# Splitting four state steps of a scan into three fp32r passes, and moving three pieces of work between engines

## The reference, cut to what matters

```
x[t] = A^T x[t-1] + B^T u[t]          u = layernorm(h), t = 0..511 in each sequence
c[t] = max |x[t]| over a head's 64 states
y[t] = (x[t] * e^2 / c[t]) C + u[t] D
```

## Time and profile before

| | us |
|---|---|
| median of 3 executions (lowest, highest) | 171.67 (171.63, 171.71) |
| the profiled execution's own time | 171.82 |
| its span | 170.1 |
| PE busy in the span | 161.4 |
| DVE, ACT, POOL busy | 127.9, 102.1, 101.8 |

### The profile page before, as it was taken

The page is one execution under the profiler, slowest core; times in us unless marked ns, Lnnn a source line. Parts: engine busy times, 40 slices in busy tenths (PEclk is TensorE's granted clock), DMA queues, the critical chain, the costliest instruction groups (busy, mean ns, idle before and its releaser), DMA issues.

```text
span 170.1 us, 3494 instructions
## 1 busy us (share of the span) xinstructions
PE 161.4 (95%) x1165; PEld 138.8 (82%) x1165; DVE 127.9 (75%) x403; ACT 102.1 (60%) x238; POOL 101.8 (60%) x168
## 2 busy tenths in 40 slices
PE   5988989999999999999999989999999999989992
PEld 1676875887766799987679889999999999979991
DVE  3969959833338384897994997989979898649883
ACT  3048999462134532423435857959779597788991
POOL 5337687669997035361313694996979969785000
PEclk9999999999999999999999999999999999999999
DMA  4996000000000000000000000010010100110022
GB/s 144 354 428 287 4 0 2 0 6 0 0 0 0 4 0 0 0 6 0 0 0 0 4 0 0 0 67 0 0 67 0 64 4 0 62 62 6 0 105 82
DMA packets 2182, 7.47 MB, mean 44 GB/s; under 512 B 238, under 2 KB 748, under 8 KB 1908
## 3 DMA queue, kind: packets, MB, share of 16 engines
q1 hardware_dynamic: 2146, 7.23, 11.2%
q10 hardware_dynamic: 18, 0.02, 0.1%
HBM read 5.15 MB, written 2.10 MB: 43 GB/s over the span
## 4 chain that ended last, share of the span: by engine, by line
PE 83%; ACT 5%; POOL 4%; DVE 3%; issue 3%; DMA 1%; POOLq 0%; ACTq 0%; DVEq 0%
PE bank L1347 12%; PE bank L1327 12%; PE bank L1276 8%; PE bank L1191 6%; PE bank L1185 5%; PE bank L1273 4%; PE bank L1056 4%; PE bank L1106 4%; PE bank L1081 4%; PE bank L1296 4%; PE bank L1112 3%; PE bank L1303 2%; POOL rstd L521 2%; PE bank L1029 2%; POOL hid_p L538 2%
## 5 line engine op out<-in xcount | busy, mean ns | idle before, releaser
L538 POOL TENSOR_TENSOR hid_p<-hid_f,hid_p 128x256 fp32r<-128x256 f32 x48 | 34.2, 736 | 13.6 <-ACT hid_p L696 13.6
L694 ACT ACTIVATE hid_f<-bank,pa 128x256 f32<-128x256 f32 x64 | 30.8, 492 | 16.0 <-PE bank L1327 14.1
L1327 PE MATMUL bank<-xaT_p,fc_p 128*128 128x256 f32 x192 | 35.1, 294 | 0.2 <-issue 0.2
L1347 PE MATMUL bank<-hid_p,out_hi 128*128 128x256 f32 x128 | 32.5, 290 | 1.0 <-POOL hid_p L538 1.0
L1327 PEld LDWEIGHTS bank<-xaT_p,fc_p 128*128 128x128 f32 x192 | 26.7, 190 | 0.4 <-issue 0.4
L1347 PEld LDWEIGHTS bank<-hid_p,out_hi 128*128 128x128 f32 x128 | 23.4, 188 | 2.0 <-POOL hid_p L538 1.4
L696 ACT ACTIVATE hid_p<-bank,pa 128x256 fp32r<-128x256 f32 x48 | 23.4, 488 | 0.0
L1276 PE MATMUL bank<-pb,xh 128*128 128x128 f32 x128 | 19.5, 275 | 0.0
L521 POOL TENSOR_TENSOR rstd<-spread,neg_half 128x8 f32<-128x8 f32 x8 | 13.6, 1697 | 9.5 <-DVE spread L966 9.5
L1347 PE MATMUL bank<-hid_p,out_lo 128*128 128x256 f32 x64 | 17.9, 279 | 0.0
L1276 PEld LDWEIGHTS bank<-pb,xh 128*128 128x128 f32 x128 | 16.9, 192 | 0.0
(11 more groups left out here) (161 smaller groups left out, 375.7 us busy)
## 6 DMA issues: line engine op xcount, KB each, us to landing
fc_w<-in_fc SPq DMA_DIRECT2D x2, 2048.0 KB, 11.4
out<-res SPq DMA_DIRECT2D x7, 256.0 KB, 2.0
pa<-in_pack_a SPq DMA_DIRECT2D x1, 407.0 KB, 3.2
pb<-in_pack_b SPq DMA_DIRECT2D x1, 384.0 KB, 4.5
out<-res SPq DMA_DIRECT2D x2, 128.0 KB, 1.7
pw<-in_pack_a SPq DMA_DIRECT2D x1, 64.0 KB, 3.1
emb_w<-in_emb SPq DMA_DIRECT2D x1, 62.5 KB
conv_w<-in_conv ACTq DMA_DIRECT2D x1, 1.0 KB
```

What stands on the lines that cost most here:

```text
L538: nc.gpsimd.tensor_tensor(hid_p[1][:, half, c, :], hid_f[:, m % HID_SLOTS, :], hid_p[0][:, half, c, :].bitcast(F32), ALU.subtract).then_in ...
L694: full = nc.scalar.activation(hid_f[:, m % HID_SLOTS, :], src, ACT.Gelu, bias=bias)
L1327: last = mm(fc1_bank(8 * b + n)[:, 0:HALF], fc1_p[w][:, e * HID + c * P:e * HID + (c + 1) * P], xaT_p[m][:, b % 2, half, :], start=(k == 0 ...
L1347: last = mm(out_bank(b, half)[:, half * HALF:(half + 1) * HALF], out_p[w][:, e, c * CH:(c + 1) * CH], hid_p[m][:, half, c, :], start=(c == ...
```

## The change

It does five things. (1) Group 0's state steps with q >= 1 (n = 2 to 5) become three fp32r passes; their low-part pass alone waits for the low part of the state. (2) For this ACT copies the bank of states 0 to 3 twice, first to a high part, then to X; DVE subtracts the low part from X; A is split once (ACT high, DVE low). The parts lie in slots of `out_hi` and `out_lo` that fused weights fill later. (3) u's four high parts of group 1 go from POOL to ACT, ahead of `next_starts`. (4) DVE's four `split_low` of group 1 are interleaved with the four `state_low`. (5) `fuse(3)` goes from behind group 0's state steps to between the second and the third of them; its copies on ACT go behind the second state copy.

```
-            -3: (("fuse",), ("run", "run"), ("run", "run"), ("fuse",), ...
+            -3: ((), ("run", "run"), ("run", "run"), ("fuse",), ...
# POOL
-                pool.wait_ge(fc1_split, NE)
-                pool.wait_ge(uT_ready, NB)
-                for b in range(GB):
-                    nc.gpsimd.tensor_copy(u_split(1, 0)[:, b], uT[:, GB + b]).then_inc(u_hi[1], 1)
# ACT
                 def copy_state(g, n):
                     q, a = divmod(n, NP)
                     act.wait_ge(state_done[g], n + 1)
+                    if g == 0 and q < RUN - 2:
+                        nc.scalar.activation(state_split(a, 0), scan_bank(a), ACT.Copy).then_inc(s_hi, 1)
                     nc.scalar.activation(every_run(g, a, q + 1), ..., ACT.Copy).then_inc(x_ready[g], 1)
...
+                split_a()
                 copy_out_prep(N_PREP - 1)
                 copy_runs(1, 0)
                 for e in range(2, FUSED_FRONT):
                     copy_fused(e)
+                act.wait_ge(fc1_split, NE // 2)
+                for b in range(GB):
+                    nc.scalar.activation(u_split(1, 0)[:, b], uT[:, GB + b], ACT.Copy).then_inc(u_hi[1], 1)
                 next_starts(0)
                 for n in range(NP * (RUN - 1)):
                     copy_state(0, n)
+                    if n == NP - 1:
+                        copy_fused(FUSED_FRONT)
# DVE
                 def split_low(g, b):
                     dve.wait_ge(u_hi[g], b + 1)
+                    if g == 1:
+                        dve.wait_ge(fc1_split, NE)
...
-                for n in range(GB):
-                    split_low(1, n)
+                def state_low(n):
+                    q, a = divmod(n, NP)
+                    dve.wait_ge(s_hi, n + 1)
+                    dve.wait_ge(x_ready[0], n + 1)
+                    nc.vector.tensor_tensor(state_split(a, 1)..., every_run(0, a, q + 1),
+                                            state_split(a, 0)..., ALU.subtract).then_inc(s_lo, 1)
+                dve.wait_ge(a_hi, 1)
+                nc.vector.tensor_tensor(a_split(1), a1, a_split(0).bitcast(F32), ALU.subtract).then_inc(a_lo, 1)
+                state_low(0)
+                state_low(1)
+                split_low(1, 0)
+                state_low(2)
+                split_low(1, 1)
+                state_low(3)
+                split_low(1, 2)
+                split_low(1, 3)
# PE
-                    mm(scan_bank(a), a1, every_run(g, a, q), start=False, stop=True).then_inc(state_done[g], 1)
+                    if g == 0 and q >= 1:
+                        pe.wait_ge(a_lo, 1)
+                        pe.wait_ge(s_hi, n - 1)
+                        for k, (w, m) in enumerate(PARTS):
+                            if m == 1:
+                                pe.wait_ge(s_lo, n - 1)
+                            last = mm(scan_bank(a), a_split(w), state_split(a, m), start=False, stop=(k == len(PARTS) - 1))
+                    else:
+                        last = mm(scan_bank(a), a1, every_run(g, a, q), start=False, stop=True)
+                    last.then_inc(state_done[g], 1)
...
                 state_step(0, 1)
+                fuse(FUSED_FRONT)
                 for n in range(NP, NP * (RUN - 1)):
                     state_input(0, n)
                     state_step(0, n)
```

More of the change, by code:

```diff
@@ L227, in build @@
         next_ready = [sem(f"next_ready{g}") for g in range(NG)]
+        a_hi, a_lo, s_hi, s_lo = sem("a_hi"), sem("a_lo"), sem("s_hi"), sem("s_lo")
         full_ready = sem("full_ready")
@@ L312, in u_runs_split, with state_split, a_split @@
             return u_split(g, part)[:, :, q:q + T - RUN + 1:RUN, :]
+        def state_split(a, part):
+            return out_p[1][:, NE - 2 * NP + 2 * a + part, :]
+        def a_split(part):
+            return out_p[0][:, NE - 1, part * P:(part + 1) * P]
         def b_split(part, a, n):
@@ L338, in build @@
         PLAN = {
-            -3: (("fuse",), ("run", "run"), ("run", "run"), ("fuse",), ("carry",), ("fuse",), (), (), ()),
+            -3: ((), ("run", "run"), ("run", "run"), ("fuse",), ("carry",), ("fuse",), (), (), ()),
             -2: (("carry",), ("carry",), ("carry", "fuse"), ("carry",), ("input", "carry"), (), ("carry", "input"),
@@ L357, in numbered @@
         def numbered(plan):
-            done, out = dict(fuse=FUSED_FRONT, run=RUN, carry=0, input=0, step=0), {}
+            done, out = dict(fuse=FUSED_FRONT + 1, run=RUN, carry=0, input=0, step=0), {}
             for j, places in plan.items():
@@ L606, in split_high, with split_a @@
                         nc.scalar.activation(u_split(0, 0)[:, b], uT[:, b], ACT.Copy).then_inc(u_hi[0], 1)
+                def split_a():
+                    nc.scalar.activation(a_split(0), a1, ACT.Copy).then_inc(a_hi, 1)
                 act.wait_ge(ld_pa, 32)
@@ L865, in _ @@
                         fused_lo((3, 4, 8).index(n))
-                for n in range(GB):
-                    split_low(1, n)
+                def state_low(n):
+                    q, a = divmod(n, NP)
+                    dve.wait_ge(s_hi, n + 1)
+                    dve.wait_ge(x_ready[0], n + 1)
+                    view = "p (b r k) -> p b r k"
+                    nc.vector.tensor_tensor(state_split(a, 1).rearrange(view, b=GB, k=NCH), every_run(0, a, q + 1),
+                                            state_split(a, 0).bitcast(F32).rearrange(view, b=GB, k=NCH),
+                                            ALU.subtract).then_inc(s_lo, 1)
+                dve.wait_ge(a_hi, 1)
[8 more added lines that the diff above has]
+                split_low(1, 3)
                 def scan_part(j, place):
```

## The result

| | before | changed |
|---|---|---|
| median of 16 executions each, us (lowest to highest) | 171.69 (171.47 to 172.08) | 172.36 (171.74 to 172.75) |
| ratio, 95% interval | | 1.0038 (1.0029 to 1.0047) |
| the profiled execution's own time, us | 171.82 | 172.38 |

The change made the kernel slower by 0.65 us (0.50 to 0.81).

What follows compares the result with a forecast made beforehand. PE's own work and few stalls bound the kernel. The last state step shifts by 0.89 for fuse(3), less 0.62 saved by four steps, plus a 0.035 stall: +0.31 us, giving 172.0 us against the median; range 171.6 to 172.5.

Steps and rivals of the forecast that it cites:

- Three passes for fp32: Group 0's state steps on PE: three fp32r passes take 0.705 us instead of 0.86, so four steps save 0.62 us.
- Three quarters: Rival for PE's state steps: passes run at 0.215 us, four steps save 0.86 us, time 171.8 us; chance 0.12.
- fuse(3) moved ahead of E5: On PE between the second and third state steps: fuse(3) hides nothing there and makes the last step end 0.89 us later.
- E5: End of group 0's last state step on PE, 57.21 us before the change, forecast at 57.525 us.
- Two copies on ACT per state: ACT behind each state step: X comes 0.49 us later, which stalls PE's input 4 by 0.035 us.
- Fused copies on ACT: fuse(3)'s two copies behind the second state copy: ACT is free again before step 2 ends, cover 0.3 us.
- Low parts on DVE: DVE's state_low and split_low subtractions: they end in time, near 57.8 us, with cover of 0.4 to 0.5 us.
- Low parts come late: Slower rival: DVE's eight subtractions and POOL hold each other off; first run pass +1.7 us, time 173.4 us; chance 0.18.
- The sum: All terms up to the end of group 0's last state step: 57.525 against 57.21 us, +0.31 us.
- What follows keeps its distances: Everything behind group 0's last state step, from run pieces through group 1, shifts equally, with hardly slack to absorb +0.31 us.
- Absorbed: Rival: a later stall, such as PE's 0.84 us at 92 to 100 us, takes in the shift; 171.7 us; chance 0.10.
- The stall behind E5 doesn't show: Faster rival: run pieces aren't held by the sixth state copy, first pass 0.64 us earlier, time 171.0 us; chance 0.05.

## Why the prediction was right, and what it missed

- **Three passes for fp32** held: 0.68 to 0.71 a step, 0.705 taken. At three quarters of the fp32 step it would be 0.645, so the rival *Three quarters* is out.
- **fuse(3) moved ahead of E5** held: +0.89 alone, and the run pieces start 0.67 behind the last step with nothing between, where 0.69 was the earlier trace rows.
- **Two copies on ACT per state**: input 4 is stalled by 0.05 (0.75 instead of 0.70), 0.035 was worked out; with X copied first it takes 0.70. What the prediction didn't price, because fuse(3) covers it, is the stall at input 2; the run with fuse(3) behind shows it.
- **Fused copies on ACT** and **u's high parts on ACT** cost nothing. ACT's timeline in the changed kernel:

```profile
47.20 2.18 ACT L654 ACTIVATE hid_p<-uT 128x512 fp32r<-128x512 f32 x4
...
49.99 0.60 ACT L597 ACTIVATE out_lo<-bank 128x512 fp32r<-128x512 f32 x1 [0.31 <-PE bank L1232]
...
52.52 0.62 ACT L586 ACTIVATE hid_f<-bank 128x512 f32<-128x512 f32 x1
53.35 0.60 ACT L597 ACTIVATE out_lo<-bank 128x512 fp32r<-128x512 f32 x1 [0.21 <-PE bank L1230]
```

  ACT waits for PE in both places, for 0.31 and 0.21 us: those are the covers left, 0.3 each by the prediction.
- **Low parts on DVE** held, and the rival *Low parts come late* didn't come. DVE's timeline in the changed kernel:

```profile
50.20 0.88 DVE L892 TENSOR_TENSOR out_hi<-pa,out_hi 128x128 fp32r<-128x128 f32 x1
...
55.94 0.69 DVE L887 TENSOR_TENSOR out_lo<-X,out_lo 128x512 fp32r<-128x512 f32 x1
56.55 1.29 DVE L799 TENSOR_TENSOR hid_p<-uT,hid_p 128x512 fp32r<-128x512 f32 x2
58.33 1.30 DVE L964 TRANSPOSE_TENSOR_REDUCE amax<-X 128x16 f32<-128x512 f32 x2 [0.50 <-ACT X L598]
```

  The subtractions of 512 columns take 0.68 to 0.72, and the last ends at 57.84 (57.8 forecast). POOL's timeline in the same stretch:

```profile
49.66 1.27 POOL L502 TENSOR_TENSOR fc_p<-fc_w,fc_p 128x512 fp32r<-128x512 f32 x1
53.28 1.43 POOL L509 TENSOR_TENSOR out_lo<-hid_f,out_hi 128x512 fp32r<-128x512 f32 x1 [2.35 <-ACT hid_f L586]
```

  POOL does nothing else between 50 and 60 us, so the rival had little to work with. DVE's subtraction for A, beside the first of these, takes 0.88 us for 128 columns; POOL's second one starts while a subtraction of DVE runs (52.87 to 53.55) and takes 1.43 instead of 1.27 to 1.29. The rule of the Trainium skill that spoke against the change ("SBUF — State Buffer", Practical consequences) agrees with these two rows, but neither instruction stands in the chain of waits.
- **The sum**, E5 +0.31: measured +0.27 to +0.29 at the last state copy in all six runs that have these steps with fuse(3) ahead. This part of the forecast came out.
- **What failed is the step "What follows keeps its distances"**, and with it the rival *Absorbed*. Behind E5 the kernel wasn't the same program any more: 13 VectorE records more moved the places where that engine pauses between two instructions. One of 0.12 us on PE's way disappeared (-0.15), one of 0.35 appeared on the way of the last sequence (+0.40). So "slower by 0.2%" became slower by 0.38%, clear of the 0.2% that the prediction called the least that can be told from no change; its likeliest outcome, the same (0.52), didn't come. That the time lies in the range at all is in part luck: the prediction had neither term, and with 7 records more the same work measures 1.0016, or +0.27 us, close to its 0.3. Of the 0.65 us measured, 0.53 are seen by 149 us; the rest is within the scatter of the last stretch. *Absorbed* came in part, for another reason: not slack that takes in a shift, since +0.89 passes through that stretch undiminished, but a pause that went.
- *The stall behind E5 doesn't show* is out: the first run pass waits for the sixth copy, as its chain has it.

Not settled is what VectorE waits for in the pause. The view of transfers by queue shows one packet of the kind "instruction" on queue 14 between 149.5 and 150.5 us in the changed kernel:

```profile
q14 instruction: 1, 0.01, 3.2%
```

The kernel before has none between 148 and 151 us, and with 13 instructions more it has one there. The packets show whose program it is. In the three kernels that differ only in VectorE's idle waits, with 500, 507 and 513 records, one packet goes from 153.15 to 152.69 and 149.52 us and one from 76.04 to 72.68 and 65.05, while the one at 126.82, 126.60 and 126.52 stays, but for the start. And packet and pause go together: in all six traces with the pause of 0.35 us a packet starts 0.65 to 0.67 us behind the start of `spread`, and in the two traces with 500 records one starts 0.65 and 0.67 us behind the end of the pause of 0.12 us (75.39 in the kernel before, 76.86 in the one with the move alone). So a piece of VectorE's program is brought in where the pause is. But it is moved behind it, so it can't itself be what VectorE waited for. The Trainium skill ("Runtime: NRT & Kernel Launch", Instruction fetch mechanics) says that an engine's program is refilled in blocks while it runs, and that crossing one is "mostly hidden"; the runs agree with a price that depends on the place in the stream, and show 0.35 us that aren't hidden. That the refill is the cause is not shown.

## What to carry to other kernels

Price a moved piece of work twice: what it costs where it goes, and the wait that it covered where it was; here 0.89 against 0.62 saved. When one engine has to copy a bank twice, make first the copy that lets the bank go, and the second from the first's result. And when two versions differ by less than 0.5 us, look for idle time that an engine's own last instruction "ended": it can belong to the length of the stream and not to the work, and a few idle waits in a covered place tell which.

## What was not expected of the hardware

- VectorE paused for 0.35 us between two dependent small instructions, at a place that only the number of its earlier instructions set: present at 513 records in five different kernels, absent at 500, 507 and 520. Moved away by idle waits, it was worth 0.0022 of the time (1.0038 to 1.0016) in one kernel and 0.0032 (0.9990 to 0.9958) in another.
- A wait for a semaphore that has long its value isn't free: VectorE's record of one lasts 0.05 us, with two waits in one instruction, and in a row they start 0.10 us apart. Seven of them put in ahead of the maxima made these some 0.33 us later.
